# Row maxima from full-height products, Newton steps on another engine, and a new order of the work

## The reference, cut to what matters

```python
# x (2, 2048, 512), ctx (2, 128, 512), H = 16, hd = 32
def xattn(hs, ctx):
    q, k, v = (heads(a) for a in (hs @ Wq, ctx @ Wk, ctx @ Wv))
    q, k = layernorm(q, gq, bq), layernorm(k, gk, bk)      # over hd
    attn = softmax(einsum('bhqd,bhkd->bhqk', q, k) / sqrt(hd))
    return merge(einsum('bhqk,bhkd->bhqd', attn, v)) @ Wo
def ffn(x):
    s = x @ Win + bin_
    h = relu(s[..., None] * W1 + b1)                       # 16 per unit
    return (einsum('btmh,mh->btm', h, W2) + b2) @ Wout + bout
x = x + xattn(layernorm(x), ctx)
x = x + ffn(layernorm(x))
```

## Time and profile before

| | |
|---|---|
| three runs | 478.17, 479.64, 479.71 us; median 479.64 |
| the profiled execution | 481.05 us, of which the span of the core is 479.2 us |
| mean granted TensorE clock in it | 0.961 of full |
| TensorE matmul busy | 433.5 us, 90% of the span |
| VectorE, ScalarE, GpSimd busy | 358.1, 331.6 and 204.4 us |
| chain that ended last | PE 69%, DVE 15%, issue 5%, ACT 5%, SP's queue 4% |

### The profile page before, as it was taken

How to read it: one execution, slowest core, us unless ns; L and a number is a source line. 1 busy time by engine, 2 the same in 40 slices (tenths; PEclk the granted TensorE clock), 3 DMA queues, 4 the chain that set the end, 5 groups by cost and what they waited for, 6 DMA issues and landing times.

```text
span 479.2 us, 7952 instructions
## 1 busy us (share of the span) xinstructions
PE 433.5 (90%) x2456; PEld 279.3 (58%) x2456; DVE 358.1 (75%) x742; ACT 331.6 (69%) x633; POOL 204.4 (43%) x189
## 2 busy tenths in 40 slices
PE   5699888999999999999999999999987998799924
PEld 2386656467376737675667647664653564357712
DVE  4799796687767996799678977695788637537885
ACT  3658747896828983798559856896479639653880
POOL 3326666345514551546253643276342502057300
PEclk9999989999999999999999999999996999799975
DMA  8552685771915187516941493119700690052004
GB/s 306 153 167 68 142 211 138 170 183 33 243 33 126 33 206 168 134 46 156 215 111 28 105 269 67 27 22 234 184 5 0 168 261 16 22 162 80 1 1 175
DMA packets 25290, 58.35 MB, mean 122 GB/s; under 512 B 5921, under 2 KB 6433, under 8 KB 22177
## 3 DMA queue, kind: packets, MB, share of 16 engines
q1 hardware_dynamic: 24992, 57.58, 45.7%
q10 hardware_dynamic: 256, 0.26, 0.2%
HBM read 22.18 MB, written 8.39 MB: 64 GB/s over the span
## 4 chain that ended last, share of the span: by engine, by line
PE 69%; DVE 15%; issue 5%; ACT 5%; SPq 4%; POOL 0%; DMA 0%; DVEq 0%; ACTq 0%; POOLq 0%
PE bank L1929 33%; PE bank L2028 8%; PE bank L1935 7%; PE bank L2016 6%; PE bank L1994 4%; DVE bank L841 4%; PE bank L2096 3%; DVE mx L769 2%; ACT hid L1433 2%; PE bank L2081 2%; PE bank L2031 2%; DVE ssq L757 2%; DVE ln L665 1%; PE bank L2040 1%; PE bank L2003 1%
## 5 line engine op out<-in xcount | busy, mean ns | idle before, releaser
L769 DVE TENSOR_REDUCE mx<-bank 128x4 f32<-128x512 f32 x128 | 83.1, 684 | 22.2 <-PE bank L1994 22.0
L1353 ACT ACTIVATE prob<-bank 128x512 f32<-128x512 f32 x128 | 72.3, 596 | 31.1 <-PE bank L2016 29.1
L520 POOL TENSOR_TENSOR qt_lo<-u,qt_hi 128x512 fp32r<-128x512 f32 x32 | 41.3, 1293 | 70.5 <-ACT u L1330 70.3
L1433 ACT ACTIVATE hid<-s_in,b_col,w_col 128x256 f32<-128x256 f32 x128 | 68.2, 597 | 1.9 <-DVE s_in L821 1.5
L2028 PE MATMUL bank<-prob,v_kv 128*32 128x512 f32 x256 | 66.8, 620 | 0.1
L2031 PE MATMUL bank<-prob,den_sel 128*32 128x512 f32 x256 | 66.3, 621 | 0.0
L841 DVE SCALAR_TENSOR_TENSOR bank<-hid,w_col,bank 128x256 f32<-128x256 f32 x120 | 58.1, 485 | 6.9
L1929 PE MATMUL bank<-wq_hi,zt_hi 128*128 128x512 f32 x128 | 55.3, 432 | 3.0 <-DVE wq_lo L683 3.0
L2016 PE MATMUL bank<-q_stack,k_stack 97*128 97x512 f32 x128 | 50.8, 446 | 7.0 <-DVE att L796 5.9
L513 POOL TENSOR_TENSOR u<-u,lnq 128x512 f32<-128x512 f32 x32 | 32.9, 1050 | 53.8 <-DVE lnq L670 53.8
L525 POOL TENSOR_TENSOR at_lo<-att,at_hi 128x512 fp32r<-128x512 f32 x28 | 35.4, 1281 | 39.3 <-ACT at_hi L1405 39.3
(11 more groups left out here) (158 smaller groups left out, 899.0 us busy)
## 6 DMA issues: line engine op xcount, KB each, us to landing
q_stack<-qt_hi SPq DMA_DIRECT2D x64, 256.0 KB, 4.9
xin<-in_x_dram SPq DMA_DIRECT2D x36, 256.0 KB, 3.9
q_stack<-qt_lo SPq DMA_DIRECT2D x32, 256.0 KB, 4.7
x<-in_x_dram SPq DMA_DIRECT2D x28, 256.0 KB, 4.7
out_dram<-x SPq DMA_DIRECT2D x28, 256.0 KB, 3.3
att<-in_L_xattn_Wk_dram SPq DMA_DIRECT2D x1, 1024.0 KB, 6.5
x<-in_L_xattn_Wq_dram SPq DMA_DIRECT2D x4, 256.0 KB, 7.4
hid<-in_L_xattn_Wv_dram SPq DMA_DIRECT2D x1, 1024.0 KB, 10.2
```

Source lines behind the costliest of these rows:

```text
L520: pool.tensor_tensor(qt_lo[:, :, cols], u[:, j, :].rearrange("p (i n) -> p i n", i=HC), qt_hi[:, :, cols].bitcast(F32), ALU.subtract).then ...
L769: dve.tensor_reduce(mx[:, j, :].rearrange("p (g i) -> p i g", g=G)[:, 2 * half:2 * half + 2, 2 * r:2 * r + 2], maxs_banks[T][half][j][r][: ...
L1353: act.activation(prob[:, h % PR, :], score_bank[t][h][:, :], ACT.Exp, scale=SCALE).then_inc(exp_done, 1)
L1433: act.activation(hid[:, hh % RR, :], of_half(s_in), ACT.Relu, bias=b1_col[:, hh:hh + 1], scale=w1_col[:, hh:hh + 1]).then_inc(hid_done, 1)
```

## The change

There are three parts.

**Maxima.** `k_diag` becomes `[128, 4, 512]`: each head of a group has its own 128 columns, four heads on the diagonal of all 128 rows. `max_scores` is two matmuls of 128 rows by 512 columns, each into a bank of its own; `row_max` reads one bank with the four heads of one `i`. The DMA and the copies that fill `k_diag` write to the new places; GpSimd clears 2048 columns where it cleared 1024.

**Newton steps.** `newton1` and `newton_q` move from VectorE to GpSimd, written there with operations of one or two inputs: five for the step (VectorE had four) and two for the shift (VectorE had one). `newton2` and the keys' Newton step stay on VectorE.

**Orders.** The lists of all five queues are new, and so are the bank tables. The first `project_q` now waits for two of the four low parts of Wq in its first half, and for all four in its second.

```diff
-        k_diag = sb("k_diag", [P, HC, 2 * KV], F32R)
+        k_diag = sb("k_diag", [P, HC, G * KV], F32R)
...
-        z1_bank = banks_of([(1, 0, 5, 7)] + [(6, 7, 1, 7)] + [(6, 4, 6, 2)] + [(4, 1, 3, 1)] * 5)
+        z1_bank = banks_of([(4, 2, 6, 4)] + [(4, 6, 3, 1)] + [(1, 6, 0, 2)] + [(1, 1, 0, 0)] * 5)
...
+            def newton(buf, v, n_in, act_sem, act_value, step_sem, base):
+                w, y, a, c2 = (buf[:, n, :] for n in range(4))
+                pool.wait_ge(act_sem, act_value)
+                pool.tensor_scalar(w, v, EPS * n_in, None, ALU.add).then_inc(step_sem, 1)
+                pool.tensor_tensor(a, y, y, ALU.mult).then_inc(step_sem, 1)
+                pool.wait_ge(step_sem, base + 2)
+                pool.tensor_tensor(a, a, w, ALU.mult).then_inc(step_sem, 1)
+                pool.wait_ge(step_sem, base + 3)
+                pool.tensor_scalar(a, a, -0.5 / n_in, 1.5, ALU.mult, ALU.add).then_inc(step_sem, 1)
+                pool.wait_ge(step_sem, base + 4)
+                pool.tensor_tensor(c2, y, a, ALU.mult).then_inc(step_sem, 1)
+            def newton1(T):
+                newton(ln1, mv1[:, :, 1], 1, ln1_act, T * 2 + 2, ln1_step, T * 7)
+                pool.tensor_scalar(shift1[:, :], mv1[:, :, 0], -1.0, None, ALU.mult).then_inc(ln1_step, 1)
+                pool.wait_ge(ln1_step, T * 7 + 6)
+                pool.tensor_tensor(shift1[:, :], shift1[:, :], ln1[:, 3, :], ALU.mult).then_inc(ln1_step, 1)
+            def newton_q(T):
+                if not first(T):
+                    pool.wait_ge(un_done, T * TB)
+                newton(lnq, ssq[:, :, :].rearrange("p j h -> p (j h)"), HD, lnq_act, T * 2 + 2, lnq_step, T * 5)
...
-                dve.tensor_reduce(mx[:, j, :].rearrange("p (g i) -> p i g", g=G)[:, 2 * half:2 * half + 2, 2 * r:2 * r + 2],
-                                  maxs_banks[T][half][j][r][:, :].rearrange("p (i g n) -> p i g n", i=2, g=2), AX.X,
+                dve.tensor_reduce(mx[:, j, :].rearrange("p (g i) -> p i g", g=G)[:, 2 * half + r, :],
+                                  maxs_banks[T][half][j][r][:, :].rearrange("p (g n) -> p g n", g=G), AX.X,
                                   ALU.max).then_inc(mx_done[half], 1)
...
-                if T == 0 and j == 0 and half == 0:
-                    pe.wait_ge(wq_lo_done, C)
+                if T == 0 and j == 0:
+                    pe.wait_ge(wq_lo_done, 2 * half + 2)
...
-                for i in range(2):
-                    for r in range(2):
-                        rows = slice(2 * HD * r, 2 * HD * (r + 1))
-                        ins = pe.matmul(maxs_banks[T][half][j][r][:, 2 * KV * i:2 * KV * (i + 1)],
-                                        qt_hi[rows, 2 * half + i, j * P:(j + 1) * P], k_diag[rows, 2 * half + i, :],
-                                        start=True, stop=True)
+                for r in range(2):
+                    ins = pe.matmul(maxs_banks[T][half][j][r][:, :], qt_hi[:, 2 * half + r, j * P:(j + 1) * P],
+                                    k_diag[:, 2 * half + r, :], start=True, stop=True)
                 ins.then_inc(maxs_done[half], 1)
```

1379 lines of the change are left out of this document (689 added, 690 removed).

## The result

| | before | after |
|---|---|---|
| median of the runs | 479.64 us | 472.07 us (4 runs, 471.05 to 475.74) |
| ratio of times, from all runs rather than the two medians | | 0.9862, 95% interval 0.9835 to 0.9889 |
| profiled execution, its span | 481.05, 479.2 us | 472.13, 470.3 us |
| mean granted TensorE clock | 0.961 | 0.962 |

The change gains 7.6 us between the medians, 6.6 us by the ratio (5.3 to 7.9), and 8.9 us between the two profiled spans. The forecast was 472.7.

The account below looks back on a forecast made before the run. TensorE was taken to bound the steady stretch, VectorE other stretches where maxima wait. Maxima 0, steady Newton steps -3.4, early stretch -3.0 and end -0.5 made -6.9 us: 474.15 profiled, 472.7 median, range 468 to 477.5 (chance 0.52).

Parts of the forecast that it names:

- What bounds the kernel: TensorE bounds the steady stretch, idle 0.91 of 51 us, nearly all one max_scores wait; elsewhere TensorE is not the bound.
- Maxima, costed at 0: Full-height max_scores on TensorE: calls save 2.5 us, values' own switches cost 2.4; taken as 0, bounds -3 and +2.
- The rule of halves: Rival: full-height max_scores calls lose the tiled rate, 0.23 us each, +15 - 7, giving 488 us; chance 0.03.
- Newton steps, -3.4 in the steady part: newton1 off VectorE brings row maxima earlier, removing four 0.85 us TensorE waits: -3.4 us, bounds 0 and -4.5.
- The stretch from 52 to 74 us, -3.0: Early stretch, Newton steps off VectorE: 3.0 of TensorE's 4.7 us idle time taken back, bounds 0 and -4.7.
- GpSimd: 96 small operations at 0.15 or 0.23 us, 18 us in all, hidden ahead of project_o if each stays under 0.54 us.
- rival 3: Slower: newton1 on GpSimd's queue delays att_low and project_o waits, from 0.54 us an operation; 482 to 489 us; chance 0.14.
- The orders, -0.5 for the end: New queue orders: SP's queue costed at nothing, the newly ordered end at -0.5 us, bounds of 4 either way.
- The sum: Whole kernel: 0 - 3.4 - 3.0 - 0.5 = -6.9 us, giving 474.15 profiled and 472.7 for the median.

Follow-up runs that it names:

- b_move: Kernel before with only newton1 moved on VectorE's list, one call of row_max later in the next iteration: 475.54 us, ratio 0.9936.
- b_pool: Kernel before with newton1 and newton_q on GpSimd, newton1 ahead of add_bout; old product, other orders and banks kept: 479.96 us, ratio 1.0007.
- b_pool2: Kernel before with both Newton steps on GpSimd, newton1 behind the last add_bout, directly ahead of att_low: 477.19 us, ratio 0.9963.
- b_full_pool: Kernel before with full-height max_scores and both Newton steps on GpSimd, old orders and banks kept: 481.50 us, ratio 1.0040.
- a_keys_x: Changed kernel with two groups of the second batch's stacked keys moved behind the first and second load of x on SP's queue: 470.55 us, ratio 0.9824.
- a_dve: Changed kernel with newton1 and newton_q back on VectorE, product and orders otherwise kept: 499.34 us, ratio 1.0447.

## Why the prediction was right, point by point

**What bounds the kernel.** Right. Where TensorE is full a wait that goes shows in full: four waits of 0.85 to 0.94 us gone made the periods 1.1 to 1.2 shorter (b_move), and the steady stretch ends at 50.98 of 51 us busy.

**Maxima, costed at 0.** Right for the change as a whole, TensorE's busy time being 431.6 against 433.5 us, and for a reason that the prediction had in parts: up to 0.17 us less a call at full height (0.11 to 0.17 measured), given back at the edges. What it did not see is that the worth of the product depends on the order. In the old orders it is a draw (periods of 49.86 us with either product); in the new ones it is worth 5.0 us by the ratios, though the new orders with the old product still beat the kernel before by 0.3%. So most of the gain needs both. The rule of halves (the Trainium skill, TensorEngine Tiling (Array Packing), Theoretical Speedup, where it stands, and not in the section that the prediction names: up to twice the rate for two row tiles) would have made the tiled product the faster one; the run with it in the new orders is 5.0 us slower. The sum of the old calls is 33.3 us by its own terms, not 33, so the saving is 2.8 and not 2.5; that changes nothing in the 0.

**Newton steps, -3.4 in the steady part.** The wait was the right one, the size too small: the four periods gave 5.7 us, above the bound of 4.5. The step that was mis-sized took the idle time that the view of waits names, 0.85 us a period, for all that was lost in waiting. The distances between starts give 1.1 for the same wait (51.0 against 49.9 with it gone), 4.5 in the four periods (b_move). The other 1.2 us of the 5.7 are no wait: the new orders have 1.4 us less of TensorE's work in the last of them, and more elsewhere. And the reason was half wrong. In the old orders "off VectorE" is not what helped: with the steps off VectorE and the order as before, nothing was gained (479.96), one place later on GpSimd 1.8 us were (477.19, by the ratio), and with `newton1` left on VectorE at another place 3.0 (475.54). In the new orders neither place that was tried on VectorE matched GpSimd.

**The stretch from 52 to 74 us, -3.0.** The number is near, and partly by luck. In the stretch itself TensorE's idle time fell by 2.1 us (from 4.7 to 2.6); up to the first `scores(t, 8)` it is 3.0 of idle time and 4.4 in all, the clock included, and 2.9 after the loss behind them. The cause is only partly shown. The Newton steps on GpSimd in the old orders brought nothing up to there (91.8 and 94.1 us for the first `scores(t, 8)`, 90.2 before). Up to 1.0 us is the split wait for Wq. The rest is the new order of the start, which was 7.7 us later with `newton1` on VectorE at the one place that was tried, and the clock; they were not taken apart further.

**GpSimd.** An operation of 4 elements took 0.20 to 0.23 us where I had taken 0.15, one of 64 elements 0.24 to 0.39 for 0.23. The additional busy time is 24.2 us for 18, far below the 0.54 an operation at which it would show, so rival 3 was off by its price. Its mechanism is real all the same: `newton1` ahead of `add_bout` delayed VectorE by 1.72 us a period (b_pool), and one place further down the queue that wait was gone (b_pool2). What decided was not the length of one operation but the whole of it, a wait of 0.86 us for ScalarE and 1.7 us of work, with urgent work behind.

**The orders, -0.5 for the end.** This is the term that was furthest off. From block 5 on the time fell by 0.2 us, and that includes the 1.3 by which the period from block 5 to 6 grew. But with the other two parts in place the orders are worth 8.5 us (b_full_pool against the change), which is more than the whole gain of 6.6: the prediction booked it under the Newton steps and the start, and those steps alone, in the old orders, brought nothing. So the total is right with the causes in part at the wrong place, and that is luck. What was costed at nothing was SP's queue: there the new order pays 1.5 us at 103 us, and the run a_keys_x gives 1.4 of them back.

**The sum.** -6.9 was forecast for the profiled execution and 8.9 came; from median to median it is 7.6, and the forecast of 472.7 lies 0.6 from the median. The terms that were too small (by 2.3 in the periods, by 1.4 at the start) and the one that was missed (1.5 on SP's queue) partly cancel.

## What to carry to other kernels

Before moving small operations to another engine, look at what stands behind them on their list and what runs beside them: moving five operations by a few calls on the same engine gave 3.0 us, moving them to an engine with time to spare gave none, because urgent work stood behind them there too. A tile shape is to be priced with its neighbours: the same product was worth nothing in one order and 5 us in another. A wait of TensorE is to be priced with its clock: of 4.9 us that a period lost by a wait of 2.6 us, some 1.6 are the clock's (a_dve). And a transfer that nobody needs soon belongs behind the ones that are waited for, at a point where its queue waits anyway.

## What the runs showed of the hardware

- A VectorE operation of 128x4 with all its operands in SBUF takes 0.15 to 0.17 us while GpSimd is idle, and 0.5 to 1.2 us, up to the end of the GpSimd operation, while that one runs with two inputs (one of 128x64 took 2.79 beside one of 4.58). The row maxima, which read PSUM, keep their length beside the same operations (four in 2.48 us in b_move). The Trainium skill (GPSIMD Engine Reference, Key points) says that the two engines share SBUF interfaces when a VectorE instruction has two SBUF inputs or works in a 2-port mode; the trace agrees. It also shows a long `TENSOR_SCALAR` with one tensor input (1.20 us at 131.08), and doesn't tell whether that one was in such a mode.
- TensorE's granted clock was at its lower level, 1.2 GHz, for most of the time from 136 to 140 us in a_dve (mean 0.59), right behind a wait of 2.80 us, and over that period TensorE was busy 2.0 us longer for the same work. Behind the single wait of 1.54 us in the change, at 105 us, it stayed at 1.00.
- The reverse was hardly seen: of GpSimd's 96 small operations two are long (0.72 us for 4 elements and 0.55 for 64), and its 128x512 subtraction keeps 1.28 to 1.31 us.
- A dependent chain of small operations on GpSimd goes on every 0.28 us, on VectorE every 0.20.
- Two executions of nearly the same kernel differ by 1.5 us and more in their first 90 us, with the granted clock (0.98 and 0.95 where they differ by 2.3 us), and in the periods behind 319 us (46.4 to 50.3 us for the one from block 5 to 6 among the variants of the change). Differences of that size between single profiles show nothing by themselves.
